# A conditioned grouped FFN whose output projection becomes seven quarter products per token pair, with its means and its condition's product computed in another place

## The chip, the cores and the metric

The kernel runs on one core of a Trainium2 chip. The metric is the device time of one execution in microseconds (us); the kernel before takes 706.3 us, the median of 3 runs (706.07 to 706.33). All tensors are float32. The matrix products are made of float32r operands: each value is split into a rounded part (`hi`) and a rest (`lo`), and a product is hi x hi + hi x lo + lo x hi, so three matmuls stand for one.

## What is computed

`x` is [4, 1024, 1024]: 4096 tokens of 1024 features, in 8 groups of 128. Shapes: W1 [8, 128, 512], W2 [8, 512, 128], emb_W [1024, 2048], out_W [1024, 1024].

```python
xr = x.reshape(B, T, 8, 128)
h = gelu(einsum('btel,elf->btef', xr, W1) + b1)          # exact gelu
y = (einsum('btef,efl->btel', h, W2) + b2).reshape(B, T, 1024)
eo = silu(cond) @ emb_W + emb_b                          # cond is [4, 1024]
scale, shift = split(eo[:, None, :], 2, axis=-1)
hn = layernorm(y, ln_g, ln_b) * (1 + scale) + shift      # over the 1024 features
out = x + silu(hn) @ out_W + out_b
```

## The kernel before

Every engine has its own program, written out by hand; semaphores join them, and the order of each queue is the order of the code. SyncE (SP) issues nearly all DMAs.

**FFN stage.** 32 items (`ORDER`), each one group g and one batch row t of 1024 tokens: groups 0 to 3 over all rows first, then row by row the groups 4 to 7. An item has four steps c, so there are M = 128 steps m. In step m TensorE runs `first(m + 2)` (W1 x tokens, 3 x 2 matmuls of 512 columns, L923) and then `second(m)` (W2 x gelu, as many, L939). ScalarE runs gelu from PSUM (L489), rounds `g_hi` in half the steps (L495), rounds x (L466) and weights, and brings each item's y out of PSUM (`stage_y`, L502), which SP stores to `y_scratch` in DRAM. VectorE rounds the other `g_hi` (L663) and forms `g_lo` (L665) and `xT_lo` (L653). In between VectorE computes the condition's product silu(cond) @ emb_W as dot products along rows: 64 half-row dots for the first two batch rows (L685), and 32 more in the projection stage (`tail_sum`, L698). The projection's weights are split into `oW_hi` and `oW_lo` (L481, L629), and the first two token pairs are normalized in the last items.

**Projection stage.** 16 pairs p of 2 x 128 tokens. y of a pair is loaded from `y_scratch` as `yb` [128 features, 8 groups, 256 tokens]. VectorE sums it over groups (L738 to L748), GpSimd's PARTITION_ALL_REDUCE gives the mean (L427), VectorE centres (L753), ScalarE squares (L509), VectorE sums (L758 to L766), GpSimd reduces (L434), ScalarE takes the root (L523), VectorE the reciprocal (L770) and the product (L775), ScalarE silu with the condition's scale and shift (L589) and the rounding (L514), VectorE the rest (L793). `project(q, g)` (L949) does one 128-token tile q: 8 groups x 3 parts x 2 halves of 512 columns, 48 matmuls into two PSUM banks. VectorE adds the sum to `res` (L868), which holds x and, added by an accumulating DMA of GpSimd (L440), the bias. SP stores `res`. Tiles alternate between two pairs of banks, and TensorE waits before tile q for the addition of tile q - 2. The last tile's product is cut into pieces (L1001).

Of the kernel before, what the change touches and what calls it, by code (L numbers as in the profile page):

```python
# [5 lines left out]
P = 128  # L6
F32 = mybir.dt.float32
# [4 lines left out]
BANK = 512  # L12
# [3 lines left out]
def cond_ffn_program(nc, x, xT, vectors, cond, W1, W2, emb_T, out_W, out_b, out):  # L16
# [40 lines left out]
    SUMS = NE * EARLY * 2  # L60
    assert B == 4 and NE == 16 and K == 1024
    DOTS = {(3, 0): 1, (15, 0): 3, (15, 1): 3}
    for n in range(4, 22):
        if n != 15:
            DOTS[n, 0], DOTS[n, 1] = (2, 3) if n in (17, 18, 20) else (1, 2)
    assert sum(DOTS.values()) == SUMS


    IN_OUT = 8
    PIECES = ((1, slice(0, IN_OUT, 2), None), (2, slice(1, IN_OUT, 2), None),  # L70
              (5, slice(8, 12), 104), (7, slice(12, 14), 0), (9, slice(14, NE), 120))
    PIECE_LOAD = {n: k for k, (n, _, _) in enumerate(PIECES)}
    PIECE_OF = {q: k for k, (_, cut, _) in enumerate(PIECES) for q in range(NE)[cut]}

    Y_SUMS = 14 * EARLY * 2
    MOD_ITEM = 22


    TAIL = []
    for q in range(8):  # L80
        TAIL += [(8 + q, (2, 3)), (q, (2,))]
    TAIL += [(q, (3,)) for q in range(8)]
    TAIL_DOTS = [(l, q, b) for l, (q, bs) in enumerate(TAIL) for b in bs]
    TAIL_SUMS = NE * (B - EARLY)
    assert len(TAIL_DOTS) == TAIL_SUMS

# [966 lines left out]
```

## Time and profile before

| | |
|---|---|
| time, median of 3 runs | 706.3 us (706.07 to 706.33) |
| span of the profiled execution | 704.15 us, so 2.15 us under the median |
| TensorE matmuls | 700.5 us busy, 99% |
| VectorE | 603.7 us, 86% |
| ScalarE | 469.3 us, 67% |
| GpSimd | 104.1 us, 15% |
| mean granted TensorE clock | 0.999 |
| DMA | 133.22 MB, 189 GB/s in the mean |

A matmul's duration in the trace includes its drain, which overlaps the next one; the step from one start to the next tells what a matmul costs. The same holds, by some 0.08 us, for VectorE's operations. Until 349 us the FFN stage runs, from there to 701 us the projection.

### The profile page before, as it was taken

To read this page: it belongs to the slowest core of one execution; us is meant where nothing else is said; L and a number is where in the kernel's file an instruction comes from. 1 tells how busy PE (TensorE), PEld (TensorE's weight loads), DVE (VectorE), ACT (ScalarE), POOL (GpSimd) and SP (SyncE) were. 2 spreads that over 40 slices of the span, in tenths; PEclk is the share of its full clock that TensorE was granted. 3 is DMA by queue.
4 is the path that set the end of the run, shared out by engine and by line. 5 is a ranking of instruction groups with operands and counts; after the bars stand their busy time and mean duration, and the time that the engine had idled before them with its cause. 6 is when DMAs were issued, how large, how long until landed. Compare 5 with 4: busy or idle time off the path is not lost.

```text
span 704.2 us, 8302 instructions
## 1 busy us (share of the span) xinstructions
PE 700.5 (99%) x3082; PEld 577.9 (82%) x3082; DVE 603.7 (86%) x725; ACT 469.3 (67%) x526; POOL 104.1 (15%) x68
## 2 busy tenths in 40 slices
PE   9999999999999999999999999999999999999998
PEld 6888888888888888888888888888888888888887
DVE  6888999999999989899887999999999978677512
ACT  7898888888878879888883456454656454555500
POOL 0000000000000011100121332423232432322100
PEclk9999999999999999999999999999999999999999
DMA  6766557344232531332789687887699877565531
GB/s 240 247 232 207 187 203 231 109 169 150 90 121 90 209 120 61 120 107 104 210 293 301 183 279 233 275 256 246 219 293 264 256 217 210 183 176 143 156 120 60
DMA packets 51880, 133.22 MB, mean 189 GB/s; under 512 B 4096, under 2 KB 25216, under 8 KB 49408
## 3 DMA queue, kind: packets, MB, share of 16 engines
q1 hardware_dynamic: 46944, 115.79, 46.9%
q0 software_dynamic: 4608, 16.78, 12.3%
q8 instruction: 24, 0.39, 0.2%
q10 hardware_dynamic: 288, 0.13, 0.1%
q14 instruction: 16, 0.13, 0.1%
HBM read 82.35 MB, written 33.55 MB: 165 GB/s over the span
## 4 chain that ended last, share of the span: by engine, by line
PE 99%; DMA 0%; ACT 0%; DVE 0%; issue 0%; DVEq 0%
PE psum L949 48%; PE psum L939 25%; PE psum L923 25%; PE psum L1001 2%; DMA wraw<-in_W 0%; PE psum L971 0%; ACT W L534 0%; DVE res L901 0%; DVEq L125 0%
## 5 line engine op out<-in xcount | busy, mean ns | idle before, releaser
L665 DVE TENSOR_TENSOR g_lo<-g_raw,g_hi 128x1024 fp32r<-128x1024 f32 x128 | 158.4, 1239 | 27.9 <-ACT g_hi L495 25.3
L489 ACT ACTIVATE g_raw<-psum,cols 128x1024 f32<-128x1024 f32 x128 | 142.9, 1116 | 34.1 <-PE psum L923 24.9
L949 PE MATMUL psum<-oW_hi,s_lo 128*128 128x512 f32 x496 | 152.7, 389 | 0.0
L949 PE MATMUL psum<-oW_hi,s_hi 128*128 128x512 f32 x496 | 152.7, 389 | 0.0
L949 PE MATMUL psum<-oW_lo,s_hi 128*128 128x512 f32 x496 | 152.6, 389 | 0.0
L939 PE MATMUL psum<-g_hi,W 128*128 128x512 f32 x512 | 136.8, 389 | 0.0
L923 PE MATMUL psum<-xT_hi,W 128*128 128x512 f32 x508 | 135.8, 389 | 0.0
L939 PEld LDWEIGHTS psum<-g_hi,W 128*128 128x128 f32 x512 | 96.1, 188 | 20.0
L923 PEld LDWEIGHTS psum<-xT_hi,W 128*128 128x128 f32 x508 | 95.3, 188 | 19.8
L949 PEld LDWEIGHTS psum<-oW_hi,s_hi 128*128 128x128 f32 x496 | 93.1, 188 | 19.4
L949 PEld LDWEIGHTS psum<-oW_hi,s_lo 128*128 128x128 f32 x496 | 93.1, 188 | 19.3
L949 PEld LDWEIGHTS psum<-oW_lo,s_hi 128*128 128x128 f32 x496 | 93.1, 188 | 19.3
L589 ACT ACTIVATE yb<-yb,mod_c,mod_a 128x256 f32<-128x256 f32 x120 | 62.3, 590 | 56.6 <-DVE yb L775 56.6
L427 POOL PARTITION_ALL_REDUCE mean_all<-mean_total x16 | 41.2, 2576 | 384.0 <-DVE mean_total L748 384.0
L939 PE MATMUL psum<-g_lo,W 128*128 128x512 f32 x256 | 78.8, 389 | 0.0
L868 DVE TENSOR_TENSOR res<-psum,res 128x1024 f32<-128x1024 f32 x31 | 37.8, 1219 | 47.6 <-PE psum L949 47.6
L923 PE MATMUL psum<-xT_lo,W 128*128 128x512 f32 x254 | 78.2, 389 | 0.0
L495 ACT CAST g_hi<-g_raw 128x1024 fp32r<-128x1024 f32 x63 | 66.3, 1052 | 8.1 <-PE psum L939 6.7
L509 ACT ACTIVATE sq<-yb 128x1024 f32<-128x1024 f32 x32 | 34.0, 1062 | 36.6 <-DVE yb L753 35.6
L434 POOL PARTITION_ALL_REDUCE var_all<-var_total x16 | 35.8, 2237 | 144.0 <-DVE var_total L766 144.0
L698 DVE SCALAR_TENSOR_TENSOR tail_out<-tail_cols,tail_cond 128x1024 f32<-128x1024 f32 x32 | 52.4, 1666 | 4.6 <-DMA tail_cols<-in_emb_T 4.6
L939 PEld LDWEIGHTS psum<-g_lo,W 128*128 128x128 f32 x256 | 47.9, 188 | 10.1 <-DVE g_lo L665 0.2
(77 smaller groups left out, 679.8 us busy)
## 6 DMA issues: line engine op xcount, KB each, us to landing
y_scratch<-y_stage SPq DMA_DIRECT2D x32, 512.0 KB, 3.1
yb<-y_scratch SPq DMA_DIRECT2D x16, 1024.0 KB, 4.8
res<-in_x SPq DMA_DIRECT2D x32, 512.0 KB, 6.1
res<-out_b_all POOLq DMA_DIRECT2D x32, 512.0 KB, 4.5
xT_raw<-in_xT SPq DMA_DIRECT2D x31, 512.0 KB, 4.3
out<-res SPq DMA_DIRECT2D x31, 512.0 KB, 4.1
tail_cols<-in_emb_T SPq DMA_DIRECT2D x24, 512.0 KB, 7.2
wraw<-in_out_W SPq DMA_DIRECT2D x16, 256.0 KB, 4.9
```

Source lines behind the costliest of these rows:

```text
L427: nc.gpsimd.partition_all_reduce(mean_all[:], mean_total[:], P, bass.bass_isa.ReduceOp.add).then_inc(mean_done, 1)
L434: nc.gpsimd.partition_all_reduce(var_all[:], var_total[:], P, bass.bass_isa.ReduceOp.add).then_inc(var_done, 1)
L489: nc.scalar.activation(g_raw[:, m % 2], ring(m), ACT.Gelu, bias=cols[:, R_B1 + k:R_B1 + k + 1]).then_inc(gelu_done, 1)
L495: nc.scalar.copy(g_hi[:, m % 2], g_raw[:, m % 2]).then_inc(ghi_act, 1)
L509: nc.scalar.activation(sq[:, half_of(h)], yb[p % 3][:, half_of(h)], ACT.Square).then_inc(squared, 1)
L589: nc.scalar.activation(yb[p % 3][:, g], yb[p % 3][:, g], ACT.Silu, scale=mod_a[:, b, g:g + 1], bias=mod_c[:, b, g:g + 1]).then_inc(silu_do ...
L665: nc.vector.tensor_tensor(g_lo[:, m % 2], g_raw[:, m % 2], g_hi[:, m % 2].bitcast(F32), ALU.subtract).then_inc(glo_done, 1)
L698: nc.vector.scalar_tensor_tensor(tail_out[i % 2][:], tail_cols[l % SLOTS][:], 1.0, tail_cond[:, b - EARLY], ALU.mult, ALU.mult, accum_out= ...
L868: nc.vector.tensor_tensor(res[:, q % 4], proj(q), res[:, q % 4], ALU.add).then_inc(out_ready, 1)
L923: mm = nc.tensor.matmul(ring(m)[:, half], W[:, g % WS, w, cut], v[:, n % 2, half], start=(k == 0), stop=(k == 2))
L939: mm = nc.tensor.matmul(y_psum(n)[:, half], W[:, g % WS, w, cut], v[:, m % 2, half], start=(c == 0 and k == 0), stop=(c == C - 1 and k == 2))
L949: mm = nc.tensor.matmul(proj(q)[:, half], v[:, g, cut], w[:, g, half], start=(g == 0 and k == 0), stop=(g == G - 1 and k == 2))
```

## The change

Three things are changed together.

**Projection.** A pair's product, [256 tokens x 1024] times [1024 x 1024], is seen as a 2 x 2 block product: tokens halves (128 each), feature halves (4 groups each), output column halves (512 each). Strassen's scheme in Winograd's form computes it as seven products of quarters. Each is [128 x 512] times [512 x 512], 4 groups x 3 parts = 12 matmuls of 512 columns. Four sums of quarters of the silu's output (`sums12`, `sum3`, `sum4`) and four sums of quarters of out_W (T1 to T4, GpSimd, `sum_o`) are made for it. P1, P6, P7 and P4 grow in one bank (`z_ps`), P5 and P3 in another, and P2 has a third; after each product VectorE adds the bank as it stands to a half row of `res` (`add`), and TensorE waits for this addition (`added`) before the bank's next product. The quarter weights that don't fit in SBUF during the FFN stage go through `wc_scratch` in DRAM.

**Means.** GpSimd issues, for each item, a DMA that adds the staged y to `y_sum` in DRAM (the first of a row writes, the later ones accumulate, each waiting for the one before). The mean's reduce reads this sum; VectorE's own sums L738 to L748 go.

**Condition.** emb_W is loaded as it is, 8 MB in items 1 to 4, and TensorE multiplies it with silu(cond), [1024 x 4], in a visit after step 24: 8 x 4 float32 matmuls with 4 output rows each, in four partition groups of one bank. The rows go through DRAM to become columns. All dots of VectorE go.

```diff
+    y_sum = nc.dram_tensor("y_sum", [NP, P, TP], F32, kind="Internal").ap()
+    wc_scratch = nc.dram_tensor("wc_scratch", [3, 2, P, HG, BANK], F32, kind="Internal").ap()
...
@@ SP @@
+                if 1 <= n <= KC // 2:
+                    for k in range(2 * (n - 1), 2 * n):
+                        sp.dma_start(emb_raw[:, k], emb_W[k]).then_inc(emb_landed, 16)
...
+            sp.wait_ge(glo_done, M)
+            load_wc(C_T3, HI, t3)
+            sp.wait_ge(s2_done, M)
+            load_wc(C_B22, HI, b22)
+            load_wc(C_B22, LO, b22)
+            load_wc(C_T4, LO, t4)
...
@@ GpSimd @@
+                nc.gpsimd.tensor_tensor(t1_raw, b12, b11, ALU.subtract).then_inc(o_sum, 1)
+                nc.gpsimd.tensor_tensor(wc_raw[:, C_T3, LO], b22_raw, b12, ALU.subtract).then_inc(o_sum, 1)
...
+            def add_y(n):
+                pool.wait_ge(y_staged, n + 1)
...
+                    pool.wait_ge(y_summed[t], 16 * k)
+                    pool.dma_start(place, part, accum_op=ALU.add).then_inc(y_summed[t], 16)
...
+            for p in range(NP):
+                if p + 2 < NP:
+                    var_of(p + 2)
+                if 1 <= p and p + 3 < NP:
+                    mean_of(p + 3)
+                if p + 1 < NP:
+                    add_bias(2 * p + 2)
+                    add_bias(2 * p + 3)
...
@@ ScalarE, after the FFN's steps @@
+            nc.scalar.preload_act_table(ACT.Silu)
+            act.wait_ge(mod_step, 6)
+            silu(1, 0)
+            stage_y(N - 1)
+            round_d(0, 2)
...
@@ VectorE @@
+                if (n, c) == (VISIT, 3):
+                    dve.wait_ge(cond_done, 1)
+                    nc.vector.tensor_copy(rows_sb[:], psum[:, VISIT_BANK]).then_inc(cond_evicted, 1)
...
+            def add(p, j, ps, t, part, of=None):
+                s = (2 * p + t) % 4
+                dve.wait_ge(prod_done, 7 * p + j)
+                dve.wait_ge(res_biased[s], 16 * ((2 * p + t) // 4 + 1))
...
+                nc.vector.tensor_tensor(res[:, s, part], ps, res[:, s, part], ALU.add).then_inc(added, 1)
...
@@ TensorE @@
+                if m == C * (VISIT + 1):
+                    pe.wait_ge(cond_evicted, 1)
...
+            def condition():
+                pe.wait_ge(cond_step, 2)
+                pe.wait_ge(emb_landed, 16 * KC)
+                pe.wait_ge(y_staged, VISIT)
+                for k in range(KC):
+                    for j in range(4):
+                        mm = nc.tensor.matmul(psum[32 * j:32 * j + B, VISIT_BANK], cond_s[:, k],
+                                              emb_raw[:, k, j * BANK:(j + 1) * BANK], start=(k == 0), stop=(k == KC - 1))
...
+            def product(to, hi, lo, w_hi, w_lo, low_ready, begin=True, passes=range(3), cut=slice(0, BANK)):
+                for k in passes:
+                    v, w = ((hi, w_hi), (hi, w_lo), (lo, w_hi))[k]
+                    if k == 2:
+                        pe.wait_ge(*low_ready)
+                    for g in range(HG):
+                        mm = nc.tensor.matmul(to[:, cut], v[:, g], w[:, g, cut], start=(begin and k == 0 and g == 0),
+                                              stop=(k == 2 and g == HG - 1), skip_group_check=not begin)
...
-                    for g in range(1 if q == 0 else 0, G):
-                        if t == 0 and g % HG == 0:
-                            pe.wait_ge(slo_done, 2 * i + g // HG + 1)
-                        project(q, g)
+                product(y2_ps, hi[0][:, s], lo[0][:, s], wa[:, A_B21, HI], wa[:, A_B21, LO], (dlo_done, 3 * p + 1))
+                pe.wait_ge(dhi_done, 3 * p + 2)
+                pe.wait_ge(added, 7 * p + P1)
+                product(z, hi[1][:, f], lo[1][:, f], wa[:, A_T2, HI], wa[:, A_T2, LO], (dlo_done, 3 * p + 2), begin=False)
...
+            for k in range(2):
+                product(last_ps[k], a_hi[p % 2], a_lo[p % 2], t4[HI], t4[LO], (alo_done, NP),
+                        cut=slice(k * TP, (k + 1) * TP))
```

The order of the products in a pair is P1, P2, P6, P5, P7, P3, P4.

VectorE, the second half of a pair and the next one's beginning, before (L793 is the rest of the silu, L698 a dot of the condition, L868 the addition to `res`):

```order
L793 TENSOR_TENSOR s_lo_88<-yb_91,s_hi_87 128x1024 [waits shi_done]
L698 SCALAR_TENSOR_TENSOR tail_out_96,emb_dots<-tail_cols_101,tail_cond 128x1024 [waits tail_landed3,tail_dot]
L868 TENSOR_TENSOR res<-psum,res 128x1024 [waits res_biased0,proj_done]
L753 SCALAR_TENSOR_TENSOR yb_90<-mean_all,yb_90 128x1024 [waits mean_done] x2
L793 TENSOR_TENSOR s_lo_88<-yb_91,s_hi_87 128x1024 [waits shi_done]
L758 TENSOR_TENSOR sq<-sq 128x1024 [waits squared]
L762 TENSOR_TENSOR sq<-sq 128x512 [waits var_tree]
L766 TENSOR_TENSOR var_total<-sq 128x256 [waits var_done,var_tree]
```

The same engine in a pair of the changed kernel, from the addition of P4 of the pair before to that of P6 (L852 is the addition to `res`, `d_raw`, `d_hi`, `d_lo` the quarters' sums and their parts, `a_lo` the rest of the quarter that needs no sum):

```order
L852 TENSOR_TENSOR res<-psum,res 128x512 [waits res_biased1,prod_done]
L813 TENSOR_TENSOR d_lo_93<-d_raw_97,d_hi_89 128x1024 [waits s_sum,dhi_done]
L765 TENSOR_TENSOR sq<-psum,sq 128x1024 [waits squared]
L852 TENSOR_TENSOR res<-psum,res 128x512 [waits res_biased2,prod_done]
L769 TENSOR_TENSOR sq<-sq 128x512 [waits var_tree]
L773 TENSOR_TENSOR var_total<-sq 128x256 [waits var_done,var_tree]
L801 TENSOR_TENSOR d_lo_94<-yb_82,d_hi_90 128x1024 [waits dhi_done]
L852 TENSOR_TENSOR res<-psum,res 128x512 [waits added,res_biased2,prod_done]
L825 TENSOR_TENSOR d_raw_99<-yb_82 128x512 [waits prod_done,silu_done]
L827 TENSOR_TENSOR d_raw_99<-d_raw_99,yb_82 128x512 [waits s_sum]
L806 TENSOR_TENSOR a_lo_102<-yb_82,a_hi_100 128x512 [waits ahi_done]
L852 TENSOR_TENSOR res<-psum,res 128x512 [waits res_biased2,prod_done]
```

One 1024-wide addition per tile has become 512-wide ones after every product, and the operations between them are fewer and smaller; the mean's sums and the dots are gone.

GpSimd where the FFN stage ends, before (L434 and L427 are the two reduces, L440 the bias):

```order
L434 ISA var_all<-var_total 128x256 [waits var_tree]
L434 ISA var_all<-var_total 128x256 [waits std_done,var_tree]
L440 DMA res<-out_b_all 128x1024 [waits res_landed0,out_b_landed]
L440 DMA res<-out_b_all 128x1024 [waits res_landed1]
L427 ISA mean_all<-mean_total 128x256 [waits centred,mean_tree]
```

And in the changed kernel (L431 is `add_y`, L449 the bias, L437 and L444 the reduces):

```order
L431 DMA y_sum<-y_stage 128x4x256 [waits y_summed3,y_staged]
L437 ISA mean_all<-sum_in 128x256 [waits centred,sum_landed]
L431 DMA y_sum<-y_stage 128x4x256 [waits y_summed3,y_staged] x3
L449 DMA res<-out_b_all 128x1024 [waits res_landed0,out_b_landed]
L449 DMA res<-out_b_all 128x1024 [waits res_landed1]
L444 ISA var_all<-var_total 128x256 [waits std_done,var_tree]
```

The first two biases now stand behind the last item's `add_y`, which waits for the last `stage_y`; before, they waited only for the residual and the bias to land.

TensorE at the end of step 24 in the changed kernel (L1006 is the second layer, L1017 the condition's product, L988 the first layer); before, L923 follows L939 there directly:

```order
L1006 MATMUL psum<-g_lo,W 128x512 [waits glo_done]
L1006 MATMUL psum<-g_lo,W 128x512
L1017 MATMUL psum<-emb_raw,cond_s 4x512 [waits y_staged,emb_landed,cond_step]
L1017 MATMUL psum<-emb_raw,cond_s 4x512 x31
L988 MATMUL psum<-xT_hi,W 128x512 [waits gelu_done]
```

The whole product stands in one piece between two steps.

## Rows read from the trace of the kernel before

**Rows 1.** The page: span, busy time of the engines, ending chain by line

```profile
span 704.2 us, 8302 instructions
...
PE 700.5 (99%) x3082; PEld 577.9 (82%) x3082; DVE 603.7 (86%) x725; ACT 469.3 (67%) x526; POOL 104.1 (15%) x68
...
PE psum L949 48%; PE psum L939 25%; PE psum L923 25%; PE psum L1001 2%; DMA wraw<-in_W 0%; PE psum L971 0%; ACT W L534 0%; DVE res L901 0%; DVEq L125 0%
```

**Rows 2.** Windows, one FFN, one projection: busy us (instructions) by engine

```profile
44.00:88.00 44.00, 44.00 (x196) 36.43 (x195) 40.04 (x56) 37.36 (x41) 0.00 (x0) 1.00 0.54 181
440.00:484.00 44.00, 44.00 (x195) 36.43 (x195) 43.66 (x47) 22.75 (x30) 14.09 (x8) 1.00 0.81 253
```

**Rows 3.** Timeline of TensorE: start us, us, engine, line, operation, count

```profile
440.05 0.62 PE L949 MATMUL psum<-oW_hi,s_hi 128*128 128x512 f32 x2
...
461.81 0.62 PE L949 MATMUL psum<-oW_hi,s_hi 128*128 128x512 f32 x2
```

**Rows 4.** Timeline of VectorE in the projection, columns as above

```profile
445.12 1.21 DVE L868 TENSOR_TENSOR res<-psum,res 128x1024 f32<-128x1024 f32 x1
446.26 1.74 DVE L770 RECIPROCAL psum<-std 128x256 f32<-128x256 f32 x1
448.03 2.35 DVE L775 TENSOR_TENSOR yb<-yb,psum 128x1024 f32<-128x1024 f32 x2
450.30 1.22 DVE L738 TENSOR_TENSOR sq<-yb 128x1024 f32<-128x1024 f32 x1
451.56 0.69 DVE L744 TENSOR_TENSOR sq<-sq 128x512 f32<-128x512 f32 x1
452.28 0.42 DVE L748 TENSOR_TENSOR mean_total<-sq 128x256 f32<-128x256 f32 x1
452.62 1.22 DVE L793 TENSOR_TENSOR s_lo<-yb,s_hi 128x1024 fp32r<-128x1024 f32 x1
453.76 2.12 DVE L698 SCALAR_TENSOR_TENSOR tail_out<-tail_cols,tail_cond 128x1024 f32<-128x1024 f32 x1
...
467.08 1.21 DVE L868 TENSOR_TENSOR res<-psum,res 128x1024 f32<-128x1024 f32 x1
```

**Rows 5.** Timeline of VectorE in the FFN stage: two 512-wide operations

```profile
45.12 0.68 DVE L629 TENSOR_TENSOR W<-wraw,W 128x512 fp32r<-128x512 f32 x1
45.73 0.68 DVE L685 SCALAR_TENSOR_TENSOR dot_out<-emb_out,cond_all 128x512 f32<-128x512 f32 x1
```

**Rows 6.** Timeline of GpSimd in the projection: two of the reduces

```profile
452.81 2.69 POOL L427 PARTITION_ALL_REDUCE mean_all<-mean_total  x1 [7.10 <-DVE mean_total L748]
...
588.83 1.79 POOL L434 PARTITION_ALL_REDUCE var_all<-var_total  x1 [6.84 <-DVE var_total L766]
```

**Rows 7.** ScalarE's groups by form: count, busy us, mean ns, idle before

```profile
L514 ACT CAST s_hi<-yb 128x1024 fp32r<-128x1024 f32 x32 | 33.7, 1053 | 0.9
```

**Rows 8.** Timeline where the FFN ends: last first-layer slots, last gelu

```profile
348.48 0.62 PE L923 MATMUL psum<-xT_lo,W 128*128 128x512 f32 x2
...
349.13 1.12 ACT L489 ACTIVATE g_raw<-psum,cols 128x1024 f32<-128x1024 f32 x1 [0.67 <-PE psum L923]
```

**Rows 9.** Line L440, the bias: issue ns min/median/max; time to landing

```profile
L440 POOL DMA_DIRECT2D res<-out_b_all x32: 859/908/1037, 341.1 to 674.7; - x32
...
DMA to landing us min/median/max: 4.4/4.5/9.7
```

**Rows 10.** Windows at the end: busy us by engine, PEclk, DMA share, GB/s

```profile
701.00:702.00 1.00, 0.41 (x4) 0.20 (x2) 0.71 (x3) 0.00 (x0) 0.00 (x0) 1.00 0.00 0
703.00:704.20 1.20, 0.00 (x0) 0.00 (x0) 0.00 (x0) 0.00 (x0) 0.00 (x0) 0.64 0.11 30
```

**Rows 11.** Line L957, the start-up's float32 matmuls: ns min/median/max

```profile
L957 PE MATMUL psum<-const-float32-0.0 x4: 671/1061/1193, 0.8 to 3.5; 128*128 128x512 f32 x4
```

**Rows 12.** DMA issues: count, KB each, median us from issue to landing

```profile
xT_raw<-in_xT SPq DMA_DIRECT2D x31, 512.0 KB, 4.3
...
emb_out<-in_emb_T SPq DMA_DIRECT2D x2, 2048.0 KB, 10.3
```

**Rows 13.** Line L466: ScalarE's idle time before it, us and times

```profile
  DMA xT_raw<-in_xT: 3.0, 4
```

More of the change, by code:

```diff
@@ L63, in cond_ffn_program @@
[L63 to L85, printed above, removed]
-    AHEAD = {q: 3 if q % 2 else 1 for q in range(1, 13)}
-    AHEAD.update({14: 1, 15: 2, 16: 1, 17: 2, 18: 1, 19: 1})
-    assert sum(AHEAD.values()) == TAIL_SUMS and sum(v for q, v in AHEAD.items() if q < 13) == 24
@@ L418, in _ @@
+            for s in range(3):
+                sp.wait_ge(out_stored[s], 16 * (QN // 4))
             sp.wait_ge(out_stored[3], 16 * (QN // 4 + 2))
@@ new lines, in _ @@
+                if (n, c) == (30, 2):
+                    sums12(0)
+                if (n, c) == (30, 3):
+                    rest_a22(0)
+                if (n, c) == (31, 1):
+                    sum3(0)
+                    sum4(0)
+                    rest_d(0, 1)
+            left, right = slice(0, BANK), slice(BANK, D)
+            for p in range(NP):
+                if p >= 1:
+                    add(p - 1, P4, z_ps(p - 1), 1, left)
+                rest_d(p, 2)
+                if p + 2 < NP:
+                    var_sum_first(p + 2)
+                add(p, P1, z_ps(p), 0, left)
+                if p + 2 < NP:
+                    var_sum_rest(p + 2)
+                if p + 1 < NP:
+                    rest_d0(p + 1)
+                add(p, P2, y2_ps, 0, left, of=P1)
+                if p + 1 < NP:
+                    sums12(p + 1)
+                    rest_a22(p + 1)
+                add(p, P6, z_ps(p), 0, right)
+                if p + 3 < NP:
+                    centre(p + 3, 0)
+                    centre(p + 3, 1)
+                add(p, P5, y5_ps, 1, right)
+                if p + 2 < NP:
+                    invert(p + 2, rstd_ps, std_ps)
+                if p + 1 < NP:
+                    sum3(p + 1)
+                add(p, P7, z_ps(p), 1, right, of=P5)
+                if p + 2 < NP:
+                    norm(p + 2, 0, rstd_ps)
+                if p + 1 < NP:
+                    sum4(p + 1)
+                add(p, P3, y5_ps, 0, right, of=P6)
+                if p + 2 < NP:
+                    norm(p + 2, 1, rstd_ps)
+                if p + 1 < NP:
+                    rest_d(p + 1, 1)
@@ L904, in _ @@
+            p, s = NP - 1, (QN - 1) % 4
+            nc.vector.tensor_tensor(res[:, s, left], z_ps(p), res[:, s, left], ALU.add).then_inc(added, 1)
+            for k in range(2):
+                part = slice(k * TP, (k + 1) * TP)
+                add(p, P4 + k, last_ps[k][:, part], 1, part, of=P4)
         @block.tensor
```

968 lines of the change are left out of this document (502 added, 466 removed).

## The prediction

> **What bounds the kernel now.** I read the page first. TensorE is busy 99% of the span and the three matmul lines L949, L939 and L923 are 98% of the chain that ended last [rows 1]: the time is the number of matmul slots times the length of a slot. Then the timeline, for the slot. Between 440.05 and 461.81 us stand 48 rows of two 512-column matmuls, so a slot is 21.76 / 96 = 0.2267 us, at the full granted clock (2.4 GHz) [rows 2, 3]. A pair of 128-token tiles takes 2 x 8 x 3 x 2 = 96 slots, 21.76 us. Then I asked which engine comes next, stage by stage. In the FFN stage VectorE is busy 40.0 of 44 us and ScalarE 37.4; in the projection VectorE is busy 43.7 of 44, ScalarE 22.8 [rows 2]. The starts of VectorE's additions into `res` two tiles apart are 467.08 - 445.12 = 21.96 us [rows 4]: it is already 0.2 us a pair slower than TensorE and falls behind, and TensorE doesn't notice because nothing in a pair waits for it closely. Any change that shortens TensorE's pair runs into VectorE at once.
>
> **TensorE's saving.** Seven products of 4 x 3 = 12 slots replace 96 slots: 84, or 19.04 us a pair. Over 16 pairs 192 slots go: 192 x 0.2267 = 43.5 us. This term I hold for sure.
>
> **VectorE's new pair.** Durations in the timeline overlap, so I count from start to start. A 1024-wide two-tensor operation steps 1.14 us (445.12 to 446.26), 1.26 where the next one needs its result; a dependent 512-wide one 0.72, a 256-wide one 0.34, and the reciprocal up to 1.77 [rows 4]. A 512-wide one with nothing dependent behind it steps 0.61 [rows 5]; the additions from PSUM are priced like it, since at 1024 they step 1.14 as well. The new pair has seven 512-wide additions (4.27), eight 1024-wide operations: two `rest_d`, `rest_d0`, two `centre`, two `norm`, `var_sum_first` (9.12), `rest_a22` and the four sums of quarters, one of them dependent (4 x 0.61 + 0.72 = 3.16), the variance's rest (0.72 + 0.34), and the reciprocal, about 1.70. Sum 19.31 us, already over TensorE's 19.04. What goes (the tail dots, the mean's tree) is counted as gone.
>
> **What GpSimd adds to it.** The timeline shows a 1024-wide VectorE operation of 2.12 us where others take 1.22, at 453.76, just when a PARTITION_ALL_REDUCE runs, which itself takes 2.69 us there and 1.79 at 588.83 [rows 4, 6]. So each reduce holds up for 0.9 us an operation that meets it. The new pair has two reduces, back to back. By the order, the first starts under `rest_d0`; the addition of P2, which has one operand in PSUM, covers 0.6 of its 0.9 us, and 0.4 is left for `sums12`; the second starts under `sums12` and holds up `rest_a22` for 0.9. I take 1.3 us; bounds 0 and 1.8. The Trainium skill (SBUF — State Buffer, "Who interferes with whom") says that a VectorE instruction with two SBUF inputs contends with a GpSimd instruction that reads SBUF and that one with at most one does not. The trace agrees with its first half by the 0.9 us above; by its second half the PSUM operands are free, as assumed.
>
> VectorE's pair is then 20.6 us. Does TensorE add waits of its own? Walking one pair with VectorE's clock at 0 when it begins the last pair's P4: P1 is added by 3.5, P6 may start at 3.8 and ends 2.72 later at 6.5, VectorE reaches it at about 8.6. In the same way each product is ready 0.5 to 2 us before VectorE comes to it. So VectorE sets the pair and no more is added. ScalarE, 11.4 us a pair now [rows 2], gets half a 1024-wide cast (1.05, [rows 7]) and one whole one more: about 13 us, hidden. The means need DRAM sums; their load waits only for the reduce before it and has 8 us. Pairs 0 to 12 have this full load; 13 to 15 don't and run at 19.04. The excess is 13 x (20.6 - 19.04) = 20.3, less 0.9 as pair 0 has one reduce: 19.4 us. Bounds: 13 x 0.27 = 3.5 and 13 x 2.07 = 26.9.
>
> **The seam.** Before, the first addition into `res` came 11 us after the projection's first slots. Now P1 is complete 0.9 us after the FFN's last matmul and P6 may not begin before P1 is added, since both grow in one bank; every later product stands behind P6 on TensorE. The addition waits for `res_biased`, and on GpSimd's queue the bias now stands behind the last `add_y`. Count from the end of the last first-layer slot, F (348.93 us in the trace: the row at 348.48 and two slots; its gelu starts at 349.13) [rows 8]. ScalarE: gelu and cast to F + 2.7, table load 1.3, four silu 2.1, the last `stage_y` 1.1: F + 7.2. GpSimd issues `add_y`, 0.9, then the bias at F + 8.1. A bias lands 4.4 to 9.7 us after issue, 4.5 in the median [rows 9]; with 5.5 MB of quarter weights, y and residuals issued in the same 10 us I take 7, so F + 15.1. Then 0.69 for the addition and 0.25 to start: P6 at F + 16.1. TensorE is free at F + 9.5: after F stand three second-layer blocks of 6 slots, 12 slots of P1 and 12 of P2, 42 x 0.2267. Stall 6.6 us, bounds 3.9 and 9.2. After the last matmul the granted clock fell to 0.64 on average in the last 1.2 us [rows 10], so part of P6 may run at 1.2 GHz; VectorE is late anyway then and hides it.
>
> **The condition's product on TensorE.** 32 float32 matmuls of 512 columns against a 4-column stationary operand. The one such form in the trace is the pair of start-up matmuls: each gives two records, of 1.06 us in the median and 0.67 at the shortest [rows 11]. A float32r record of 0.39 us has a slot of 0.2267, so 0.16 to 0.24 of it is drain; with the same drain a float32 record costs about 0.43 us of array time where it is short and 0.85 where it is long, which I take for the two clocks, 2.4 and 1.2 GHz. 64 records one after another are 27.5 us at the full clock. They write four different 32-partition groups in turn and leave most columns of the array empty, so the four of a k may run side by side: 6.9 us. I take 7.5 with the change of mode. The page TensorE: Matmul & The Clock Gate of the Trainium skill ("Measured speedup vs the span model") gives 2.38 for three such column tiles; no run here shows it. By that rate the product would cost about 11.5 us, an estimate from that page, and the sum would be 4 us higher. In the same visit `second(28)` waits for `cond_evicted`, and VectorE's copy stands behind `rest_x(8)` and `split_gelu(29)`: about 1.5 us late. No dots on VectorE pay for this: they were hidden under TensorE.
>
> **The rest of the FFN stage.** emb_W comes as 8 MB in items 1 to 4, 2 MB an item; a 2 MB piece takes 10.3 us to land now, beside an x tile's 4.3 [rows 12], and an item is 48 slots, 10.9 us. So the queue is nearly full there, with a y_sum write of 0.5 MB per item on top. ScalarE waits already for x, 3.0 us in four times [rows 13], without TensorE showing it. The 28 quarter casts and splits replace 16, and 64 dots go, so VectorE has more room than before; but sixteen 512-wide operations on GpSimd read SBUF. No row shows one; the nearest is the reduce's 0.9 us hold. 16 x 0.9 = 14.4 us of VectorE in all, in four bursts of 3.6, beside some 3 us of idle an item: hidden but for an edge. The load of `emb_dots` is 8192 elements of 4 bytes, priced by no row; it has 40 us until `modulation`. I take 2 us for all of this, bounds 0 and 10. The GPSIMD Engine Reference of the Trainium skill (3.1) lists a tensor_tensor on GpSimd at 1.96 times VectorE's time; by that the bursts would be some 5 us each, an estimate from it, and the edge 3 us wider. Two 256-wide halves of the last P4 and a 256-wide last store in place of two of 128: +0.3 at the end.
>
> **Sum.** The profiled execution spans 704.15 us; the median of the runs, 706.3, lies 2.15 above and I carry that over. 704.15 - 43.5 + 19.4 + 6.6 + 7.5 + 1.5 + 2 + 0.3 = 697.95, with 2.15: 700.1. I forecast 700 us. Its own range, with the contention, the bias's landing and the edge at their bounds by turns, is 692 to 708.
>
> **Rivals.** (1) The four column groups don't overlap. For it: each is two records with its own weight load, and no matmul of this trace runs beside another. Then the visit costs 27.5 in place of 7.5: 720 us, slower. It decides from a product of 13.7 us, an overlap of less than two. (2) VectorE's meetings with GpSimd are mostly free: for it, `norm`, the reciprocal and half of `var_sum_first` read PSUM, and at 588.83 a reduce took 1.79 with nobody held up [rows 6]; against it, `rest_d0` and `sums12` have both inputs in SBUF. With 0.3 us a pair of contention the excess is 13 x 0.57 = 7.4 in place of 19.4: 688 us. (3) The full queue makes x late in items 1 to 4 or the 4-byte transfer slows those of items 10 to 13, and TensorE waits for x each time, 1 us on eight items: 708 us. Against it, ScalarE's waits of now cost nothing.
>
> **Chances.** The forecast 0.50, rival 1 0.22, rival 2 0.17, rival 3 0.11. A difference under 0.2%, 1.4 us, can't be told from none here. Faster: 0.92 of the forecast, and rival 2: 0.64. Within 0.2%: 0.05. Slower: rival 1, most of rival 3 and an edge: 0.31. The range 687 to 719 takes in rival 2 and 3 and what the forecast's bounds reach; it leaves out about half of rival 1 (720, with its own spread) and little else, under 0.2.
>
> **What would show it.** In the profile after: matmuls of L1028 in steps of 0.227 within a product with gaps between products whose releaser is VectorE's `res`; a pair of 20.6 us in pairs 1 to 12 and 19.0 in the last three; VectorE at 98% or more there, with one or two operations a pair 0.4 to 0.9 us longer than their like; a gap of about 6 us before the first P6 that ends with the bias's DMA; the 64 records of L1017 in about 7.5 us. Wrong if VectorE shows idle time in the steady pairs while TensorE waits (a chain I didn't see), if L1017 takes over 14 us, or if TensorE has gaps in the first 16 items.

## The result, and the profile after

The changed kernel takes 742.84 us in the median of 4 runs (741.12 to 746.77), the kernel before 706.32. The ratio is 1.052 with a 95% interval of 1.049 to 1.055: clearly slower, where 700 us and faster was forecast. The profiled execution took 743.72 us and spans 741.70.

The page of the changed kernel, against [rows 1] (engines' busy time, then the shares of the chain that ended last):

```profile
span 741.7 us, 8277 instructions
...
PE 693.2 (93%) x2960; PEld 541.6 (73%) x2960; DVE 602.8 (81%) x663; ACT 488.9 (66%) x566; POOL 172.7 (23%) x116
...
q1 hardware_dynamic: 47760, 115.90, 46.6%
q0 software_dynamic: 19968, 33.56, 26.5%
...
DVE 34%; PE 27%; DMA 16%; issue 13%; ACT 9%; SPq 1%; DVEq 0%; POOL 0%; ACTq 0%; POOLq 0%
```

The chain was 98% TensorE's three matmul lines; now TensorE is 27% of it, and no engine replaces it: VectorE, transfers and ScalarE take turns. So the time is no longer set by one engine that is always busy, but by waits that pass from engine to engine.

Windows of the changed kernel, two of the FFN stage and one of the projection, columns as in [rows 2]:

```profile
44.00:88.00 44.00, 43.29 (x222) 30.67 (x221) 27.02 (x28) 28.02 (x29) 4.09 (x4) 1.00 0.88 269
220.00:264.00 44.00, 42.14 (x177) 32.27 (x177) 36.13 (x37) 34.49 (x38) 12.07 (x8) 1.00 0.71 179
528.00:572.00 44.00, 41.88 (x180) 33.04 (x179) 43.86 (x50) 28.21 (x37) 16.18 (x11) 1.00 0.75 210
```

In the FFN stage nobody is near full: VectorE works 36 of 44 us, ScalarE 34, and TensorE ran 177 matmuls where it ran 196. In the projection VectorE is full, as forecast.

Where the time went can be read from the starts of the second layer's groups. Before, all items lie 10.88 us apart. The table gives what the items take above that in the profiled executions, in us, and F, the end of the last first-layer slot (the start of its last matmul and 0.2267 us):

| | start to item 5 | items 6 to 8 | 9 to 19 | 20 to 30 | F | last matmul after F |
|---|---|---|---|---|---|---|
| before | 0 | 0 | 0 | 0 | 348.9 | 352.2 |
| changed | 2.4 | 13.2 | 14.6 | 15.9 | 395.0 | 343.6 |

The FFN stage is 46 us longer, the projection only 8.6 shorter.

The first cause stands in ScalarE's wait before it rounds x, against [rows 13], and in the landing times, against [rows 12]. Line L485 of the changed kernel (us, times) and two of its DMA issues (count, KB, median us to landing):

```profile
  DMA xT_raw<-in_xT: 36.8, 18
```

```profile
y_sum<-y_stage POOLq DMA_DIRECT2D x32, 512.0 KB, 8.4
...
xT_raw<-in_xT SPq DMA_DIRECT2D x31, 512.0 KB, 5.5
```

x lands 5.5 us after its issue instead of 4.3. How much of that the kernel before could take was to be had from its own timeline: the issue of an x tile on SP's queue and the rounding of that tile on ScalarE.

```profile
183.36 0.51 SPq L307 DMA_DIRECT2D xT_raw<-in_xT  x1
...
188.24 1.05 ACT L466 CAST xT_hi<-xT_raw 128x1024 fp32r<-128x1024 f32 x1
```

The rounding is due 4.9 us after the issue and x landed at 187.30, so 0.9 us are free; over items 2 to 30 this slack is 0.02 to 1 us but once. The next load can't be issued earlier, as it waits for VectorE's rest of the tile before. So x that lands 1.2 us later makes ScalarE wait for it in most items. A wait of ScalarE need not cost TensorE anything, though: how long it may be is shown by the run that puts the transfers alone into the kernel before.

The seam in the changed kernel's timeline, against [rows 8]; two DMA issues, then VectorE and TensorE:

```profile
402.74 1.28 POOL L431 DMA_DIRECT2D y_sum<-y_stage  x1 [8.97 <-ACT y_stage L528]
...
403.51 2.32 POOL L449 DMA_DIRECT2D res<-out_b_all  x2
...
421.60 0.69 DVE L852 TENSOR_TENSOR res<-psum,res 128x512 f32<-128x512 f32 x1 [16.11 <-DMA res<-out_b_all]
...
422.44 3.75 PE L1028 MATMUL psum<-wa,d_hi 128*128 128x512 f32 x8 [17.80 <-DVE res L852]
```

The wait is the forecast one, at the forecast place, but 17.8 us long instead of 6.6. Behind it eight matmuls take 3.75 us where eight take 1.98 otherwise: the granted clock is at half (1.2 GHz) after the stand. The windows at the seam (last two columns: DMA share, GB/s; PEclk ahead of them) show why the bias is late:

```profile
396.00:400.00 4.00, 4.00 (x20) 3.30 (x19) 2.73 (x4) 3.68 (x6) 0.00 (x0) 1.00 1.11 274
404.00:408.00 4.00, 0.64 (x3) 0.19 (x1) 1.49 (x2) 3.92 (x6) 1.83 (x3) 0.98 1.02 408
412.00:416.00 4.00, 0.00 (x0) 0.00 (x0) 0.00 (x0) 0.00 (x0) 0.00 (x0) 0.50 1.07 338
```

The DMA share is about 1 or above throughout: all 16 DMA engines are busy, while the other engines stand.

A pair of the projection, VectorE's rows beside GpSimd's two reduces, against [rows 4, 6]:

```profile
565.59 1.22 DVE L801 TENSOR_TENSOR d_lo<-yb,d_hi 128x1024 fp32r<-128x1024 f32 x1
566.73 0.68 DVE L852 TENSOR_TENSOR res<-psum,res 128x512 f32<-128x512 f32 x1
567.33 0.98 DVE L825 TENSOR_TENSOR d_raw<-yb 128x512 f32<-128x512 f32 x1
568.34 0.69 DVE L827 TENSOR_TENSOR d_raw<-d_raw,yb 128x512 f32<-128x512 f32 x1
568.95 1.58 DVE L806 TENSOR_TENSOR a_lo<-yb,a_hi 128x512 fp32r<-128x512 f32 x1
570.46 0.68 DVE L852 TENSOR_TENSOR res<-psum,res 128x512 f32<-128x512 f32 x1
```

```profile
565.77 2.70 POOL L444 PARTITION_ALL_REDUCE var_all<-var_total  x1 [13.51 <-DVE var_total L773]
568.37 2.32 POOL L437 PARTITION_ALL_REDUCE mean_all<-sum_in  x1
```

The addition of P6 recurs every 20.30 us (550.16 to 570.46). The two holds are on the forecast operations, 0.3 us on the first sum (0.98 in place of 0.69) and 0.9 on `rest_a22` (1.58 in place of 0.69).

The condition's product (ns min/median/max, first and last start):

```profile
L1017 PE MATMUL psum<-emb_raw,cond_s x64: 589/592/594, 78.1 to 84.6; 128*4 128x512 f32 x64
```

64 records in 6.5 us, a start every 0.10 us; step 24 is 7.3 us longer than others.

### The profile page after: what moved, and what is told of

It reads as the page before. It is cut to its first block, busy times and chain, and to the rows that moved or that the text cites. A ratio compares the mean times of both kernels' runs of the same rounds, so it can differ in the third digit from the quotient of the medians.

```text
span 741.7 us, 8277 instructions
## 1 busy us (share of the span) xinstructions
PE 693.2 (93%) x2960; PEld 541.6 (73%) x2960; DVE 602.8 (81%) x663; ACT 488.9 (66%) x566; POOL 172.7 (23%) x116
## 3 DMA queue, kind: packets, MB, share of 16 engines
q0 software_dynamic: 19968, 33.56, 26.5%
## 4 chain that ended last, share of the span: by engine, by line
DVE 34%; PE 27%; DMA 16%; issue 13%; ACT 9%; SPq 1%; DVEq 0%; POOL 0%; ACTq 0%; POOLq 0%
PE psum L1028 11%; PE psum L1006 8%; PE psum L988 7%; DMA xT_raw<-in_xT 5%; DVE res L852 5%; DMA y_sum<-y_stage 4%; ACT g_raw L514 4%; DVE yb L760 4%; DMA o_raw<-in_out_W 3%; DVE yb L782 3%; DVE d_lo L813 3%; DVE g_lo L728 3%; DVE a_lo L806 3%; DMA res<-out_b_all 2%; ACT g_hi L520 2%
## 5 line engine op out<-in xcount | busy, mean ns | idle before, releaser
L988 PE MATMUL psum<-xT_hi,W 128*128 128x512 f32 x508 | 139.8, 397 | 10.5 <-ACT g_raw L514 10.4
L1006 PE MATMUL psum<-g_hi,W 128*128 128x512 f32 x512 | 139.9, 395 | 5.8 <-DVE g_hi L726 3.3
L1028 PE MATMUL psum<-wa,d_hi 128*128 128x512 f32 x512 | 128.6, 394 | 17.8 <-DVE res L852 17.8
L1028 PEld LDWEIGHTS psum<-wa,d_hi 128*128 128x128 f32 x512 | 97.5, 191 | 38.7 <-issue 18.2
L988 PEld LDWEIGHTS psum<-xT_hi,W 128*128 128x128 f32 x508 | 95.3, 190 | 37.3 <-ACT g_raw L514 16.1
L1006 PEld LDWEIGHTS psum<-g_hi,W 128*128 128x128 f32 x512 | 96.5, 190 | 29.2 <-DVE g_hi L726 5.5
L852 DVE TENSOR_TENSOR res<-psum,res 128x512 f32<-128x512 f32 (+1 forms) x113 | 76.3, 675 | 37.3 <-PE psum L1028 20.9
L444 POOL PARTITION_ALL_REDUCE var_all<-var_total x16 | 43.6, 2723 | 211.6 <-DVE var_total L773 211.6
L1006 PE MATMUL psum<-g_lo,W 128*128 128x512 f32 x256 | 83.6, 408 | 3.0 <-DVE g_lo L728 2.5
L431 POOL DMA_DIRECT2D y_sum<-y_stage x28 | 37.8, 1350 | 189.6 <-ACT y_stage L528 189.6
L988 PE MATMUL psum<-xT_lo,W 128*128 128x512 f32 x254 | 78.9, 392 | 0.0
L1028 PE MATMUL psum<-wa,d_lo 128*128 128x512 f32 x256 | 69.3, 393 | 0.0
L1006 PEld LDWEIGHTS psum<-g_lo,W 128*128 128x128 f32 x256 | 45.5, 190 | 24.0 <-DVE g_lo L728 16.9
L485 ACT CAST xT_hi<-xT_raw 128x1024 fp32r<-128x1024 f32 x31 | 32.5, 1048 | 36.8 <-DMA xT_raw<-in_xT 36.8
L1028 PEld LDWEIGHTS psum<-wa,d_lo 128*128 128x128 f32 x256 | 48.6, 190 | 10.2
L988 PEld LDWEIGHTS psum<-xT_lo,W 128*128 128x128 f32 x254 | 48.0, 189 | 10.5
L726 DVE CAST g_hi<-g_raw 128x1024 fp32r<-128x1024 f32 x65 | 51.9, 799 | 3.8 <-PE psum L1006 3.1
```

Source lines behind the costliest of these rows:

```text
L431: pool.dma_start(place, part, accum_op=ALU.add).then_inc(y_summed[t], 16)
L444: nc.gpsimd.partition_all_reduce(var_all[:, p % 2], var_total[:], P, bass.bass_isa.ReduceOp.add).then_inc(var_done, 1)
L485: nc.scalar.copy(xT_hi[:, n % 2], xT_raw[:, n % 2]).then_inc(xhi_done, 1)
L726: nc.vector.tensor_copy(g_hi[:, m % 2], g_raw[:, m % 2]).then_inc(ghi_dve, 1)
L852: nc.vector.tensor_tensor(res[:, s, part], ps, res[:, s, part], ALU.add).then_inc(added, 1)
L988: mm = nc.tensor.matmul(ring(m)[:, half], W[:, g % WS, w, cut], v[:, n % 2, half], start=(k == 0), stop=(k == 2))
```

## The experiments

Times are medians of 4 runs, the ratio is to the kernel before on the same chip (706.5 to 706.6 us).

**The accumulating transfers left out.**

```diff
+                if k > 0:
+                    return
```

> The changed kernel without the 28 accumulating DMAs into y_sum (only the first item of each batch row writes its y there; the means are those of one group alone). In the changed kernel the first-layer slots end at 394.95 us against 348.93 before; about 34.8 of the 46.0 us arise in items 7 to 31, where ScalarE waits 30.3 us for x in 13 times. Theory A (the accumulating transfers of 512 KB, 7 us to land in the median, slow the loads of x from 4.2 to 5.5 us, and the loop load of x, rounding, rest, next load has no slack for it): the first layer ends between 360 and 370 and the time is 705 to 718 us. Rival B (the loads and stores of out_W's quarters and of emb_W, GpSimd's sums and VectorE's new order do it): the first layer still ends after 388 and the time stays above 734.

Measured: 721.41 us, ratio 1.0215 (1.018 to 1.025). F falls by 18.5 to 376.4; items 9 to 19 lose 6.9, items 20 to 30 lose 7.6. x lands in 4.2 us in the median, and ScalarE's wait for it:

```profile
  DMA xT_raw<-in_xT: 10.0, 8
```

Between the two theories: the transfers cost 21.4 us, and F falls by about half of the 34.8 us that theory A put on them; the rest of the FFN's loss has other causes. Its page gives their price on the queues as well (packets, MB, share of the 16 engines' span):

```profile
q0 software_dynamic: 5184, 18.88, 12.6%
```

26.5% of 741.7 less 12.6% of 718.7 is 106 us for 28 transfers: each takes as much time as all 16 engines have in 3.8 us.

**Plain writes in their place.**

```diff
-                    pool.dma_start(place, part, accum_op=ALU.add)
+                    pool.dma_start(place, part)
```

> The changed kernel with plain writes in place of the accumulating ones: 28 DMAs of the same bytes on the same queue, y_sum holds the last group's y alone. Theory A1 (it is the adding, a read of y_sum and a slower transfer per element, that slows x): most of the gain of the run without them, the first layer ends below 375, 710 to 725 us. Theory A2 (any 512 KB more per item beside x does it, or the issue on GpSimd): within 5 us of the changed kernel, 738 to 746.

Measured: 725.22 us, 1.027 (1.024 to 1.030), at the upper end of A1 in time; F is 382.5, over A1's 375. Of the 21.4 us, 17.6 go with the adding and 3.8 stay with the plain writes (of F's 18.5, 12.5 and 6.1). The same page row:

```profile
q0 software_dynamic: 9216, 33.56, 17.4%
```

17.4% of 724.4 is 126.0 us, so a plain write costs (126.0 - 90.6) / 28 = 1.3 us of the engines, against 3.8 for an adding one of the same size.

The edit changes a second thing with the adding. By the packets of these rows a plain write is (9216 - 5184) / 28 = 144 packets and an adding one (19968 - 5184) / 28 = 528. The 32 biases stand between: they are adding transfers of 512 KB too, but into SBUF and in 144 packets, and the kernel before has nothing else in this row:

```profile
q0 software_dynamic: 4608, 16.78, 12.3%
```

12.3% of 704.2 us over 32 is 2.7 us each. As far as transfers into SBUF and into DRAM compare, both count: the adding (1.3 to 2.7) and the many small packets (2.7 to 3.8).

**x ahead of y_sum.**

```diff
                 pool.wait_ge(y_staged, n + 1)
+                if n + 3 < N:
+                    pool.wait_ge(x_landed[(n + 3) % 2], 16 * ((n + 3 + (n + 3) % 2) // 2))
```

> The changed kernel with add_y(n) waiting until x of item n + 3, whose load is issued at about the same time, has landed: all transfers stay, their order changes. Theory A: x lands in 4.2 to 4.5 us again in the items without other loads; of the 34.8 us of items 7 to 31 more than half goes, the time is 712 to 728. Rival B: no change, 738 to 746. Rival C (the queue as a whole is full, whatever the order): the wait turns up at the staging of y or at the end, 735 or more.

Measured: 738.42 us, 1.046 (1.042 to 1.050), which overlaps the changed kernel's interval: no clear gain. The time fits B and C alike; C is what the trace shows, as x lands in 4.4 us again and the waits turn up elsewhere: items 14, 18 and 21 now lose 5.3, 3.1 and 7.9 us. In item 21 ScalarE waits 8.56 us for x, whose load stands on SP's queue behind a wait for `y_summed`:

```profile
277.77 1.04 ACT L487 CAST xT_hi<-xT_raw 128x1024 fp32r<-128x1024 f32 x1 [8.56 <-DMA xT_raw<-in_xT]
```

**The biases of pair 0 before the last add_y.**

```diff
+                if n == N - 1:
+                    pool.wait_ge(out_b_landed, 16)
+                    for q in range(2):
+                        add_bias(q)
                 add_y(n)
-            pool.wait_ge(out_b_landed, 16)
-            for q in range(2):
-                add_bias(q)
```

> The changed kernel with the biases of pair 0 issued before the last add_y instead of behind it. In the changed kernel TensorE stands from 404.5 to 422.4 until the bias has landed in res. If the position in the queue is all of it, P6 of pair 0 starts at about 407 and 15 to 18 us go: 725 to 729. If the transfers at the seam are the limit (the high part of T4 is issued only at 425.0, when the last store of y has landed at 424.9, and lands at 431.0), P4 of pair 0 waits for it instead of starting at about 418; it starts at 436.2 now, so about 5 us go: 735 to 740. I expect the second.

Measured: 747.70 us, 1.060 (1.055 to 1.064), not faster at all. The gap before P6 is 1.6 us, but a new one of 16.1 stands before P3, and it is neither of the two that I had named. VectorE's queue (in brackets the idle time before a row and what ended it):

```profile
410.87 0.68 DVE L853 TENSOR_TENSOR res<-psum,res 128x512 f32<-128x512 f32 x1
431.92 2.36 DVE L761 SCALAR_TENSOR_TENSOR yb<-mean_all,yb 128x1024 f32<-128x1024 f32 x2 [20.36 <-DMA yb<-y_scratch]
434.20 0.68 DVE L853 TENSOR_TENSOR res<-psum,res 128x512 f32<-128x512 f32 x1
```

The centring of pair 3 needs y of pair 3, loaded behind the weights, and the addition of P5 that TensorE needs is queued behind it.

**Only the y_sum transfers, in the kernel before.**

```diff
+            for n in range(N):
...
+                add_y(n)
```

> The kernel before with only one part of the change: GpSimd's DMAs that write and add each item's y into y_sum (nothing reads y_sum; the staging of y waits for them as in the changed kernel, and the biases of tile 0 and 1 stand before the last of them). If those transfers alone hold x up wherever the FFN stage has TensorE at 99%: x lands in about 5.3 us instead of 4.2 and 15 to 25 us are lost, 721 to 732. If they only cost beside the changed kernel's other transfers and its other order on VectorE: within 4 us of the kernel before, 706 to 710.

Measured: 716.44 us, 1.0147 (1.0125 to 1.017), between the two. F is 358.2, 9.3 us later. x lands in 5.3 us and ScalarE waits for it 28.3 us in all, against 36.8 in the changed kernel:

```profile
  DMA xT_raw<-in_xT: 28.3, 25
```

The transfers cost 9.9 us here and 21.4 in the changed kernel, whose FFN stage has other delays beside them. Where the 9.3 us arise says more: 3.5 up to item 5, 1.3 in items 6 to 8, 4.5 in items 20 to 30, and none in items 9 to 19, though ScalarE waits for x in each of these (its wait between 117 and 237 us: total, times, longest):

```profile
ACT xT_hi L493 <- DMA xT_raw<-in_xT: 8.4, 11, 1.4
```

TensorE has no wait at all in that stretch. So in steady items of the kernel before a wait of up to 1.4 us for x is hidden. In items 9 to 19 of the changed kernel ScalarE waits 19.6 us in nine times, up to 3.6, and 14.6 us are lost.

**The condition's rows copied three steps earlier.**

```diff
-                if (n, c) == (VISIT, 3):
+                if (n, c) == (VISIT, 0):
                     dve.wait_ge(cond_done, 1)
```

> The changed kernel with VectorE's copy of the condition's rows three steps earlier in its queue (after step 24's split instead of behind the rest of x and the split of step 29). There VectorE stands idle for 7.2 us anyway. TensorE's wait before second(28), 94.4 to 97.2, and the six slots at 1.2 GHz behind it (1.4 us) should go: 4 to 5 us, 738 to 739. If the loop around x holds that place as well, nothing: 741 to 744.

Measured: 740.02 us, 1.0465 (1.044 to 1.049). Items 6 to 8 lose 8.7 instead of 13.2 us, so by the two traces the copy's place cost 4.5; items 9 to 19 lose 3.9 more than in the changed kernel's trace, and 2.8 us remain between the medians, whose intervals touch.

**GpSimd's sums of quarters cut to 8 columns, from the kernel without the adding transfers.**

```diff
-                nc.gpsimd.tensor_tensor(t1_raw, b12, b11, ALU.subtract)
+                nc.gpsimd.tensor_tensor(t1_raw[:, 0:8], b12[:, 0:8], b11[:, 0:8], ALU.subtract)
```

> The kernel without the accumulating transfers (e1) and with GpSimd's sixteen sums of quarters of out_W cut to 8 of 512 columns, the casts and splits reading o_raw instead. In e1 items 10 to 17 lose 6.9 us. If GpSimd's hold on VectorE's two-input operations (0.7 to 1.1 us each in 9 of them) is the cause, 4 to 7 us of it go: 714 to 717. If the loads of out_W and the stores of its parts do it: 720 to 722.

Measured: 714.09 us, 1.0097 (1.008 to 1.012). 7.3 us go; items 9 to 19 lose 1.2 us instead of 6.9. The kernel leaves out most of each sum and still has every transfer of out_W, so the sums are the cause and not the loads. That casts had to wait for a sum's result is no rival: in the run without the adding transfers no wait for GpSimd stands between 100 and 245 us. The hold is plain in the changed kernel's timeline: beside these sums a `g_lo` takes 2.31 us in place of 1.22 and a weight's rest 1.78 in place of 0.69.

```profile
226.19 1.50 POOL L413 TENSOR_TENSOR wa_raw<-o_raw 128x512 f32<-128x512 f32 x1 [2.59 <-DMA o_raw<-in_out_W]
...
226.46 2.31 DVE L728 TENSOR_TENSOR g_lo<-g_raw,g_hi 128x1024 fp32r<-128x1024 f32 x1
...
227.66 2.27 POOL L414 TENSOR_TENSOR wc_raw<-o_raw 128x512 f32<-128x512 f32 x1
...
228.70 1.78 DVE L675 TENSOR_TENSOR W<-wraw,W 128x512 fp32r<-128x512 f32 x1
```

**A third of the quarter weights at the seam.**

```diff
-            load_wc(C_B22, HI, b22)
-            load_wc(C_B22, LO, b22)
-            load_wc(C_T4, LO, t4)
...
-            load_wc(C_T4, HI, t4)
```

> The changed kernel with 2 MB of quarter weights loaded at the seam instead of 6 MB (T3 stands for B22 and T4 too, so the products P3 and P4 are with the wrong quarter); the order of the queues and the place of the biases stay. If the bias's landing 17 us after its issue is a matter of bytes ahead of it: TensorE's gap before P6 of pair 0 falls from 17.8 to 3 to 7 us, 728 to 733. If it is the chain in the queues (the store of y, the last adding transfer, then the bias): it stays over 14 us, 738 to 743.

Measured: 739.57 us, 1.047 (1.0455 to 1.049). The bias still lands at 418.7, and TensorE waits 13.8 us for it, just under the 14 of the second theory. The time from the bias's issue to its landing falls from 18.0 us to 14.0, so the 4 MB are the smaller part of it and what stands in the queues beside them the larger.

**Both edits at the seam.** The two diffs above together.

> The changed kernel with both edits at the seam: 2 MB of quarter weights instead of 6 (P3 and P4 use T3's quarter) and the biases of pair 0 before the last add_y. Each alone gave nothing or 3 us: with the biases first, VectorE's centre of pair 3 waited for yb until 431.9 behind the weights and TensorE for it, 16.1 us; with a third of the weights the bias still landed at 418.8. If the two waits stand behind each other (queue and bytes), only both together free the seam: all gaps of TensorE between 400 and 440 sum to 3 to 7 us and the time is 726 to 732. If there is a third wait of the same size (the last stores of y): 737 or more.

Measured: 738.14 us, 1.045 (1.043 to 1.046). TensorE's waits between 400 and 440 us are 1.6, 2.6 and 10.2, not 3 to 7. VectorE waits 13.0 us for `yb` of pair 3 here, 20.4 with the 4 MB, so they are the smaller part of that wait. The last store of y, issued at 399.17, lands at 419.4, and the load of pair 3 issued behind it at 421.6, with the 16 DMA engines full until 420. Whether the load would land sooner without the store wasn't tried:

```profile
412.00:416.00 4.00, 2.43 (x11) 1.69 (x9) 0.00 (x0) 0.00 (x0) 0.00 (x0) 1.00 1.11 269
416.00:420.00 4.00, 0.00 (x0) 0.00 (x0) 0.00 (x0) 0.00 (x0) 0.00 (x0) 0.57 1.02 290
420.00:424.00 4.00, 0.00 (x0) 0.00 (x0) 2.38 (x3) 1.06 (x1) 0.00 (x0) 0.50 0.16 53
```

**VectorE's pair made shorter.**

```diff
+                wide = HG if p < 2 else 1
-                part = yb[p % 3][:, half_of(h)]
+                part = yb[p % 3][:, h * HG:h * HG + wide]
```

> The changed kernel with VectorE's two products with 1 over the deviation (L782) cut from 4 groups to 1 from pair 2 on (the other groups aren't scaled): about 1.7 us of VectorE less per pair. If VectorE's busy time sets the pair of 20.31 us, and TensorE's 84 slots are next, pairs 1 to 12 take 19.0 to 19.1 and 13 x 1.27 = 16.5 us go: 725 to 728. If it is a chain of waits between the products (TensorE stands 0.7 us before P7 in each pair), the pair stays over 19.8: 736 or more.

Measured: 730.41 us, 1.034 (1.032 to 1.035). TensorE has no gap after 425 us. From F to the last matmul 15.4 us go in the trace, 12.4 between the medians. The window of a steady stretch:

```profile
528.00:572.00 44.00, 44.00 (x195) 36.35 (x195) 43.32 (x55) 28.66 (x40) 13.20 (x8) 1.00 0.80 216
```

TensorE is full again and a pair is its 84 slots, 19.04 us. VectorE's work did set the pair, as forecast.

**The condition's product, one column group after the other.**

```diff
-                for k in range(KC):
-                    for j in range(4):
+                for j in range(4):
+                    for k in range(KC):
```

> The changed kernel with the condition's product in the order column group by column group (8 matmuls into one group of 32 partitions, then the next group) instead of the four groups in turn. In the changed kernel its 64 records run in 6.6 us, 0.10 apart, each 0.59 long. If the four groups run side by side because successive matmuls go to different groups, the same 64 records take about four times that, 0.41 apart, 26 us, and the time is 760 to 764 us. If small stationary operands alone make it short, it stays at 6.6: 741 to 745.

Measured: 759.59 us, 1.075 (1.072 to 1.0785), 16.75 us more.

```profile
L1017 PE MATMUL psum<-emb_raw,cond_s x64: 590/592/593, 77.8 to 99.7; 128*4 128x512 f32 x64
```

The same records start 0.35 us apart instead of 0.10, so the order of issue alone makes the four groups run side by side, by a factor of 3.4.

**The change, mended.** The early copy, the early biases, and on SP's queue the last store of y and the load of pair 3 ahead of B22 and T4.

```diff
-            sp.wait_ge(s2_done, M)
-            load_wc(C_B22, HI, b22)
-            load_wc(C_B22, LO, b22)
-            load_wc(C_T4, LO, t4)
             sp.wait_ge(y_staged, N)
...
             load_y(3)
+            sp.wait_ge(s2_done, M)
+            load_wc(C_B22, HI, b22)
+            load_wc(C_B22, LO, b22)
+            load_wc(C_T4, LO, t4)
```

> The whole change with three moves and nothing left out: VectorE's copy of the condition's rows at step 24, the biases of pair 0 before the last add_y, and at the seam the last store of y and the load of pair 3's y ahead of the parts of B22 and T4. From the copy 3 to 4 us; at the seam the biases land by 405, y of pair 3 by 412, T3 by 414, B22 by 422 and T4 by 428, so P4 of pair 0 at about 428 instead of 436: 8 us. 730 to 735. If the 10 MB of the seam come in whatever order no sooner than 431 to 434: 736 to 741. Slower than the kernel before in either case, as the adding transfers, the quarter sums and VectorE's bound stay.

Measured: 738.75 us, 1.046 (1.044 to 1.048). At the seam the last weights land at 431.0 in this order too, although F is 3.6 us earlier; TensorE now waits 12.4 us for B22 instead of 17.8 for the bias:

```profile
426.25 3.62 PE L1029 MATMUL psum<-b,d_hi 128*128 128x512 f32 x8 [12.38 <-DMA b<-wc_scratch]
```

## Why the prediction was wrong

Forecast for the profiled execution: 697.95 us of span. Measured: 741.70, so 43.7 more. Term by term:

- **TensorE's saving, -43.5: right.** 84 slots and 19.04 us a pair where VectorE lets it (the run with narrow norms).
- **VectorE's excess, +19.4: right in kind, 4 too large.** The pair was 20.30 us, not 20.6, and removing the bound gave 15.4 in the trace. Both holds by GpSimd came where they were forecast. The rule of the Trainium skill that was weighed there (SBUF — State Buffer, "Who interferes with whom") fits for the additions with one PSUM operand, which kept their 0.68 us beside the reduces. The Trainium skill says it there for at most one SBUF input only outside VectorE's 2-port modes, which the prediction left out; casts with one SBUF input were held in the FFN stage (1.58 us beside a reduce at 298.60 in place of 0.69), and no run shows their mode. Not every operation with two SBUF inputs was held: `rest_d0`, begun 0.2 us before a reduce, kept its 1.22. And the reading that at 588.83 a reduce held nobody up, on which rival 2 leaned, was wrong: beside it L721 took 1.09 us for 8 elements a partition, where L722 took 0.15 for as many.
- **The condition, +7.5: right, 7.3.** Rival 1 is excluded. The factor of 3.4 for four groups stands beside the 2.38 for three that the Trainium skill (TensorE: Matmul & The Clock Gate, "Measured speedup vs the span model") gives.
- **The late copy of its rows, +1.5: it was 4.5** by the traces (13.2 less 8.7 in items 6 to 8), 2.8 between the medians. The copy's place in VectorE's queue was seen; that TensorE came back from this stop at half the clock was left out (the next four matmuls took 2.04 us, not 1.07).
- **The rest of the FFN stage, +2 with bounds 0 and 10: this is the step that failed.** It was about 34 us: 46.0 less 7.3 and 4.5. I named both causes and priced them as hidden. The price of a y_sum transfer was its 0.5 MB; it costs the DMA engines three times a plain write of that size. The sums' hold was counted at 0.9 us each, in bursts of 3.6; the bursts lasted 6.0 to 7.5 us. And "ScalarE's waits of now cost nothing", the argument against rival 3, was true of the kernel before and was carried over to waits of another length: up to 1.4 us they are hidden (items 9 to 19 with the transfers alone), and in the changed kernel they reach 3.6 there and 5.9 in item 21. The parts of the 34 us: the adding transfers 18.5 of F (21.4 between medians), the quarter sums' hold on VectorE 6.6 (7.3). Rival 3 had the mechanism but for eight items of 1 us; the changed kernel loses time in 25 of the 31 steps from item to item, as y_sum has a transfer in every item and not only while weights are loaded. The prediction's own sign, gaps of TensorE in the first 16 items, is there. Some 9 us are left in the kernel without the transfers and the sums, 7.7 of them in items 20 to 30, where y of the first pairs is loaded and reduced. Their cause wasn't tried; six operations of VectorE are 0.6 to 0.9 us longer than their like there, beside GpSimd's reduces.
- **The seam, +6.6 with bounds 3.9 and 9.2: it was 18.0** (404.48 to 422.44), and 2.9 more since P6 and P5 ran partly at half the clock; how much of this VectorE hid, as the prediction says it would, isn't known. The bound for the bias's landing, 9.7 us [rows 9], was the longest of the kernel before, at 530 us, with the queues 0.91 full. Here their share is 0.82 to 1.11 from 396 to 432 us, and the bias landed 18.0 us after its issue (403.51 to 421.51). The experiments show three waits behind each other: the bias, y of pair 3, and the weights that land at 431. Taking away one, or two, uncovers the next. How the queues' 36 us from F to 431 divide between the weights, the store of y with its short rows and the adding transfers stays open.

Summed: 35.0 us too little in the FFN stage and 8.6 behind it make 43.6 of the 43.7. Behind F the measured terms, -43.5, 15.4, 18.0 and 2.9, give -7.2 where the trace has -8.6; the 1.4 us between aren't explained.

## What to carry to other kernels

A wait that costs nothing now shows only that a wait of its own length is free. Before traffic is added to a queue, read from the starts how long after its issue each transfer is needed, compare with its landing time, and ask how long a wait the engine behind can take; the change's traffic alone, put into the kernel before, measures it. Price an accumulating DMA by the share of the engines' time that its queue shows per transfer, not by its bytes. Where a stage starts with several late things, removing the one that ends last gives only the distance to the next, or nothing.

## What the runs showed that was not expected

- An accumulating DMA of 512 KB into DRAM took 3.8 us of the 16 engines in 528 packets, one into SBUF 2.7 us in 144, a plain write to DRAM on the same queue 1.3 us in 144.
- The same transfers, with x landing 1.0 to 1.2 us later, cost 9.9 us in one kernel and 21.4 in another that had more delays beside them; in eleven items of the first they cost nothing at all. Such costs don't add: one uses up the room that hides the other.
- A GpSimd instruction held not only two-input operations of VectorE but also the float32r cast of 1024 columns: up to 2.16 us beside `add_y` and a reduce, 0.70 at most in the kernel before.
- The changed kernel's runs spread over 5.7 us, those of the kernel before over 0.8. That the time now hangs on when transfers land would explain it; no run tests it.
